# Gated cross-attention and FFN on one core: half of the first context group loaded from ScalarE's queue, context transposed ahead of x, and every engine's order table redrawn

## What is computed

```python
def reference(x, ctx_2048, mask_BxS2_bk0, g_xattn, g_ffn, L0_ffn_w_gating, L0_ffn_w_linear):
    def _L0_xattn_ref(hidden_states, memory_tokens, memory_mask):
        scale = 1.0 / jnp.sqrt(jnp.asarray(D, hidden_states.dtype))
        scores = jnp.einsum('bsd,bmd->bsm', hidden_states, memory_tokens) * scale
        scores = jnp.where(memory_mask[:, None, :], scores, neg_inf)
        attn = jax.nn.softmax(scores, axis=-1)
        readout = jnp.einsum('bsm,bmd->bsd', attn, memory_tokens)
...
    def _L0_ffn_ref(x, w_gating, w_linear):
        ff_gate = _qdot(x, w_gating[0])
        gate_value = jax.nn.gelu(ff_gate)
        ff1 = _qdot(x, w_gating[1])
        activations = gate_value * ff1
        outputs = _qdot(activations, w_linear)
        return outputs
    x = x + jnp.tanh(g_xattn[0]) * _L0_xattn_ref(_layernorm(x, axis=-1), ctx_2048, mask_BxS2_bk0)
    x = x + jnp.tanh(g_ffn[0]) * _L0_ffn_ref(_layernorm(x, axis=-1), L0_ffn_w_gating, L0_ffn_w_linear)
    return x
```

## Time and profile before

| | us |
|---|---|
| median of 3 runs | 126.36 (126.28 to 127.42) |
| the profiled execution, time | 127.25 |
| its span, first to last instruction | 125.50 |
| PE busy | 120.9 (96%) |
| DVE busy | 97.0 (77%) |
| ACT busy | 87.8 (70%) |
| POOL busy | 82.3 (66%) |

### The profile page before, as it was taken

One profiled execution on the slowest core, in us unless ns is written; L12 is line 12 of the kernel. 1 busy time (PEld: TensorE's weight loads), 2 busy tenths in 40 slices (PEclk: granted clock), 3 DMA queues, 4 the chain that ended last, 5 costly groups with the idle time before them and its releaser, 6 DMA issues.

```text
span 125.5 us, 2568 instructions
## 1 busy us (share of the span) xinstructions
PE 120.9 (96%) x863; PEld 104.2 (83%) x863; DVE 97.0 (77%) x210; ACT 87.8 (70%) x155; POOL 82.3 (66%) x143
## 2 busy tenths in 40 slices
...
GB/s 99 320 189 334 416 290 49 94 123 229 264 291 102 159 218 130 110 81 284 356 254 102 0 0 0 130 45 0 0 0 5 0 0 0 3 0 47 42 125 125
DMA packets 34440, 15.73 MB, mean 125 GB/s; under 512 B 26230, under 2 KB 33019, under 8 KB 34427
## 3 DMA queue, kind: packets, MB, share of 16 engines
...
HBM read 14.52 MB, written 1.05 MB: 124 GB/s over the span
## 4 chain that ended last, share of the span: by engine, by line
PE 66%; SPq 11%; DMA 10%; ACT 4%; issue 4%; DVE 3%; DVEq 0%; ACTq 0%
PE ring L774 13%; SPq L369 10%; DMA cn<-in_ctx_dram 8%; PE scores L854 6%; PE pv L825 6%; PE pv L833 6%; PE pv L829 6%; PE scores L788 6%; PE scores L791 6%; PE scores L792 6%; PE ring L870 6%; DMA raw<-in_ctx_dram 2%; ACT gate L575 2%; DVE ring L639 1%; PE scores L808 1%
## 5 line engine op out<-in xcount | busy, mean ns | idle before, releaser
L461 POOL TENSOR_TENSOR chl<-cn,chl 128x256 fp32r<-128x256 f32 (+1 forms) x52 | 37.8, 761 | 7.1 <-ACT chl L519 7.0
L645 DVE TENSOR_TENSOR pT_lo<-ring,pT_hi 128x512 fp32r<-128x512 f32 (+1 forms) x32 | 17.6, 578 | 6.9 <-ACT pT_hi L512 6.7
L512 ACT ACTIVATE pT_hi<-ring 128x512 fp32r<-128x512 f32 (+1 forms) x32 | 15.6, 513 | 8.3 <-PE ring L774 8.1
L645 DVE TENSOR_TENSOR cT_lo<-ring,cT_hi 128x512 fp32r<-128x512 f32 (+1 forms) x28 | 16.8, 624 | 4.5 <-ACT cT_hi L512 4.5
L792 PE MATMUL scores<-cT_hi,xT_lo 128*128 128x512 f32 (+2 forms) x60 | 20.1, 342 | 0.0
L791 PE MATMUL scores<-cT_lo,xT_hi 128*128 128x512 f32 (+2 forms) x60 | 20.0, 342 | 0.0
L469 POOL TENSOR_TENSOR ws<-ws,wc 128x256 f32<-128x256 f32 x24 | 15.4, 674 | 6.0 <-DVE wc L687 6.0
L825 PE MATMUL pv<-chl,pT_hi 128*128 128x256 f32 (+1 forms) x104 | 18.9, 294 | 0.0
L512 ACT ACTIVATE cT_hi<-ring 128x512 fp32r<-128x512 f32 (+1 forms) x28 | 14.6, 547 | 5.3 <-PE ring L774 3.2
L833 PE MATMUL pv<-chl,pT_lo 128*128 128x256 f32 (+1 forms) x104 | 17.5, 281 | 0.0
L829 PE MATMUL pv<-chl,pT_hi 128*128 128x256 f32 (+1 forms) x104 | 17.5, 280 | 0.0
...
## 6 DMA issues: line engine op xcount, KB each, us to landing
...
out_dram<-xs SPq DMA_DIRECT2D x8, 128.0 KB, 1.7
...
```

Of the source, the lines that this page charges most:

```text
L461: last = nc.gpsimd.tensor_tensor(chl[b % 2][0:parts, t, D:2 * D], cn[b % 2][0:parts, t, :], chl[b % 2][0:parts, t, 0:D].bitcast(f32), ALU. ...
L512: nc.scalar.activation(dst, bank_view(f, size), ACT.Copy).then_inc(hi_ready, 1)
L645: nc.vector.tensor_tensor(dst, bank_view(f, size), hi.bitcast(f32), ALU.subtract).then_inc(lo_ready, 1)
```

## The change

`WARM` goes from 14 to 12. The first half of the first context group, 256 KB, is issued by ACT as its first transfer instead of by SP as its third; SP keeps the second half. PE turns `C0:0` ahead of `X0:0`. All six tables (PE, ACT, DVE, POOL, SP and the banks) are redrawn. The instructions are the same ones, except the two filler matmuls. Of the tables, the diff below shows the first line of PE's and all of SP's.

```diff
-    WARM = 14
+    WARM = 12
...
     PE_ORDER = """
-        X0:0 C0:0 W2 X0:1 C0:1 W3 A1:0 A1:1 W4 C0:2 C0:3 A0:0 B0:0 A0:1 C0:4 C0:5 B0:1 S1:1 B0:3 B0:2 C1:1
+        C0:0 X0:0 W4 X0:1 C0:1 A1:0 W2 A0:0 W3 C0:2 C0:3 A1:1 A0:1 B0:0 C0:4 C0:5 B0:1 S1:1 C1:0 C0:6 C1:1
...
     SP_ORDER = """
-        X1 C1:0 W0 M1 C1:1 C1:2 X2 C1:3 T2:0 T2:1 W1 W2 M3 C2:0 C2:1 T2:2 W3 M2 C3:3 C2:3 T3:0 T3:1 C3:0
-        C2:2 C3:1 C3:2 W4 T3:2 W5"""
+        X1 C1:0 M1 C1:3 W0 C1:1 C1:2 X2 T2:1 W1 T2:0 W2 C2:0 C2:2 C2:3 T2:2 C2:1 M3 M2 T3:0 W3 C3:1 C3:2
+        T3:1 C3:0 W4 C3:3 T3:2 W5"""
...
-                    halves = [(t0, (t0 + t1) // 2), ((t0 + t1) // 2, t1)] if b == 0 and g == 0 else [(t0, t1)]
-                    for i, (a, z) in enumerate(halves):
-                        sp_eng.dma_start(cn[b % 2][:, a:z, :], rows[:, a:z, :]).then_inc(
-                            c00_in if i < len(halves) - 1 else c_in[b % 2][g], 16)
+                    if b == 0 and g == 0:
+
+                        t0 = (t0 + t1) // 2
+                    sp_eng.dma_start(cn[b % 2][:, t0:t1, :], rows[:, t0:t1, :]).then_inc(c_in[b % 2][g], 16)
...
+            half = GT // 2
+            actor.dma_start(cn[0][:, 0:half, :], ctx_2048[0, 0:NF * P, :].rearrange(
+                "(t p) d -> p t d" if 0 in by_block else "(p t) d -> p t d", p=P)[:, 0:half, :]).then_inc(c00_in, 16)
             actor.dma_start(mrow0, mask_BxS2_bk0[0:1, :]).then_inc(m0_in, 16)
```

More of the change, by code:

```diff
@@ L62, in gated_cross_attention_ffn @@
-        P5:2 S7:1 S7:2 N0 V5:0 P5:3 P6:1 V5:1 S7:3 N1 P6:0 P6:2 V5:2 V5:3 P6:3 H0 V6:0 V6:1 P7:0 P7:1 V6:2
-        V6:3 H1 P7:3 V7:0 P7:2 V7:1 V7:2 V7:3 H2 N2 H3 H4 H5 H6 N3 H7 H8 H9 H10 H11 Y0 H12 Y1 H13 H14 H15 Y2
+        C0:0 X0:0 W4 X0:1 C0:1 A1:0 W2 A0:0 W3 C0:2 C0:3 A1:1 A0:1 B0:0 C0:4 C0:5 B0:1 S1:1 C1:0 C0:6 C1:1
+        S0:1 B0:3 S0:2 B0:2 S0:3 C1:2 X1 C1:3 S1:2 S1:3 S2:0 C1:4 C1:5 P0:0 S2:1 S3:0 P0:3 P0:1 P0:2 V0:0
+        S3:1 C1:6 S2:2 P1:0 V0:1 S2:3 P1:1 V0:2 X2 V0:3 S3:2 S3:3 P1:2 S4:0 P1:3 V1:0 V1:1 P2:0 P2:1 P2:2
@@ L64, in gated_cross_attention_ffn @@
+        V1:2 V1:3 S5:0 P2:3 S4:1 S5:1 P3:1 P3:0 V2:0 V2:1 C2:6 V2:2 V2:3 P3:3 X3 S4:2 S4:3 P3:2 V3:0 V3:1
+        V3:2 V3:3 P4:1 P4:0 S5:2 S5:3 S6:0 V4:0 C3:6 P4:2 S6:1 P5:1 V4:1 V4:2 P5:0 N0 S6:2 P4:3 S6:3 S7:0
+        S7:1 V4:3 S7:2 N1 P5:2 S7:3 P5:3 V5:0 P6:3 P6:0 P6:1 V5:1 V5:2 V5:3 H0 P7:0 P6:2 V6:0 P7:2 V6:1 V6:2
+        P7:1 V6:3 H1 P7:3 V7:0 V7:1 V7:2 V7:3 H2 N2 H3 H4 H5 H6 N3 H7 H8 H9 H10 H11 H12 H13 Y0 H14 Y1 H15 Y2
         Y3 Y4 Y5 Y6 Y7"""
     ACT_ORDER = """
-        X0:0 C0:0 X0:1 C0:1 R0:0 C0:2 C0:3 R0:1 B0:0 C0:4 C0:5 B0:1 K1 B0:3 B0:2 C1:1 C1:0 C0:6 B1 X1 C1:3
@@ L69, in gated_cross_attention_ffn @@
[L69 to L72, removed]
+        C0:0 X0:0 X0:1 C0:1 R0:0 C0:2 C0:3 R0:1 B0:0 C0:4 C0:5 B0:1 R0:2 C1:0 C0:6 C1:1 B0:3 K1 B0:2 R0:3
@@ L73, in gated_cross_attention_ffn @@
+        C1:2 X1 C1:3 E0 R1:3 C1:4 C1:5 P0:0 B1 P0:3 P0:1 P0:2 E1 C1:6 R1:2 P1:0 C2:1 K2 P1:1 C2:0 R1:0 X2 E2
+        C2:3 P1:3 P1:2 R1:1 C2:2 P2:0 P2:1 P2:2 E3 C2:5 C2:4 R2:3 P2:3 R2:2 K3 C3:0 P3:1 P3:0 B2 C2:6 R2:1
+        P3:3 R2:0 X3 P3:2 E4 C3:1 C3:2 R3:0 P4:1 R3:2 C3:3 P4:0 E5 C3:6 P4:2 L0 P5:1 C3:4 C3:5 B3 R3:1 P4:3
+        P5:0 L1 R3:3 N0 E6 P5:2 P5:3 N1 P6:3 E7 P6:1 P6:0 P7:0 P6:2 H0 P7:2 P7:1 H1 P7:3 L2 H2 N2 H3 H4 L3
         H5 H6 N3 H7 H8 H9 H10 H11 H12 H13 H14 H15"""
     DVE_ORDER = """
-        G0:0 G0:1 X0:0 C0:0 X0:1 C0:1 C0:2 C0:3 G1 C0:4 C0:5 M1:0 W0 C1:1 C1:0 C0:6 M0:0 M0:1 X1 C1:3 C1:2
@@ L78, in gated_cross_attention_ffn @@
[L78 to L82, removed]
@@ L83, in gated_cross_attention_ffn @@
-        H13 H14 Y2 H15 Y3 Y4 Y5 Y6 Y7"""
+        G0:0 G0:1 C0:0 X0:0 X0:1 C0:1 C0:2 C0:3 G1 C0:4 C0:5 M1:0 C1:0 C0:6 C1:1 M0:0 W0 M0:1 X1 C1:2 C1:3
+        M1:1 G2 C1:4 C1:5 P0:0 G3 M2:0 P0:1 P0:3 W1 P0:2 C1:6 D2:1 D2:0 P1:0 C2:1 M2:1 M3:0 C2:0 P1:1 D2:3
+        X2 A0 C2:3 P1:3 D2:2 P1:2 C2:2 M3:1 P2:0 D2:5 P2:1 P2:2 D2:4 A1 C2:4 C2:5 P2:3 D3:0 W2 C3:0 P3:1 U0
+        P3:0 M4:0 A2 C2:6 M5:0 M4:1 P3:3 X3 P3:2 D3:1 D3:2 C3:1 C3:2 A3 D3:3 P4:1 M5:1 C3:3 P4:0 U1 U3 U2
+        C3:6 P4:2 D3:4 D3:5 P5:1 C3:4 C3:5 M6:0 W3 P5:0 M6:1 P4:3 A4 M7:0 P5:2 P5:3 M7:1 P6:3 P6:0 A5 P6:1
```

14 lines of the change are left out of this document (8 added, 6 removed).

## The result

The changed kernel takes 136.15 us (136.03 to 136.29 in 4 runs); the kernel before, run beside it, takes 126.41 (126.28 to 127.42). The ratio is 1.077, with a 95% interval from 1.072 to 1.081: slower by 9.7 us. The forecast was 131.0, with 132.6 as the upper end, so the direction was right and the size was not. The profiled execution has a span of 134.5 us, against 125.5. Two single executions further down were disturbed, 307.44 us in e3 and 421.39 us in e5, and are left out of their medians.

The account below looks back on a forecast made before the run. PE was taken to bound the kernel, busy 120.9 of 125.5 us. The terms -0.6 - 0.5 + 2.7 + 2.5 + 0.5 = +4.6 on the median 126.36 gave 131.0 us, range 127.5 to 132.6.

Parts of the forecast that it names:

- head: Start of PE: first context half lands earlier, second score unit reads ready parts; -0.6 us, between 0 and -1.0.
- the stall in the middle goes: PE's wait at 64.15 ends because ACT's context group is issued before `T2:2`; -0.5 us, bounds 0 and -0.6.
- `T2:2` late: SP's block load waits for `D2:2` to free `raw`, so PE stands at `P2:3`; +2.7 us, +2.1 to +3.5.
- `T3:0` late: Next block load, behind `C2:1` and two masks, makes PE stand at `C2:6`; +2.5 us, 0 to 3.2.
- late next: `M4:0` comes late on DVE, so PE waits at `S4:2`; +0.5 us, bounds 0 and 1.1.
- everything else that moved: POOL's low parts and ACT's bias of batch 1, later now, costed at nothing because PE's work covers them.
- the upper bound: Latest landing of the first context half issued by ACT: 3.40 us after 0.72, at 4.12; head then gives 0.
- the signs: What would show the forecast in traces: DVE and PE gaps, SP's wait ending near 43, second context group near 9.2.
- One stall only: Rival, chance 0.17: `T3:0` is there in time, only the `T2:2` stall stays; +1.6, 128.0 us.
- faster or the same: Rival, chance 0.15: `T2:2` is early enough; 125.3 us without any PE stall, 126 to 127 with half stall times.
- The change doesn't do what it says: Rival, chance 0.08: shared engines bring the half no earlier, x's turn is 0.4 later; head +0.4, 132.0 us.
- The lower clock: Rival, chance 0.06: TensorE stays longer at its lower level at the head, up to 1.5 us more; 132.5 us.

Follow-up runs that it names:

- e3: Changed kernel with DVE's product `fo` written as tensor_scalar (`seen` as scalar operand) instead of tensor_tensor; 132.09 us, ratio 1.045.
- e5: Kernel before with only the new head: ACT issues the first context half, 12 fillers, `C0:0` ahead of `X0:0`; 126.44 us, ratio 1.002.
- e11: e4 with the head of before put back, so only the redrawn tables behind it are left of the change; 126.48 us, ratio 1.003.
- e4: Changed kernel with `T2:0` loaded ahead of `T2:1` on SP and `fo` as tensor_scalar; 126.63 us, ratio 1.0024.
- e3b: Same kernel as e3 in a second set of runs, made for a profile; 131.85 us, ratio 1.044.
- e8: Changed kernel with POOL waiting for its own last result behind each context group of batch 2, `fo` unchanged; 131.82 us, ratio 1.044.
- e10: Changed kernel with `T2:0` loaded ahead of `T2:1` on SP and the POOL waits of e8, `fo` unchanged; 126.30 us, ratio 1.001.
- e1: Changed kernel with only SP's two loads exchanged, `T2:0` ahead of `T2:1`; median 129.07 us, ratio 1.012 from two of six runs.
- e2: Changed kernel with SP issuing `C2:1`, `M3` and `M2` before `T2:2` instead of between it and `T3:0`; 134.88 us, ratio 1.064.
- e6: Kernel before with only ACT issuing the first context half, 14 fillers and all orders as before; 127.93 us, ratio 1.010.

## Why the prediction was wrong in size and right in direction

| step of the forecast | forecast | measured |
|---|---|---|
| head | -0.6 | -0.66 in the trace of after; 0 in the times (e5, e11 against e4) |
| the stall in the middle goes | -0.5 | -0.55 against the profiled run of before; 0 in the times |
| `T2:2` late | +2.7 | +2.95 |
| `T3:0` late | +2.5 | +2.25 |
| late next | +0.5 | +0.8 |
| everything else that moved | 0 | +2.4, and +1.6 for the lower clock behind it |

In the traces the measured terms sum to 8.8; another 0.2, in small pieces towards the end, makes the 9.0 between the spans.

**What held.** The block buffer was read rightly, down to its sizes. The wait of SP ended at 43.13 (43.2 was forecast, "near 43"), DVE stood 3.48 us before the turn from `raw` at 49.93 and 3.75 before the turn from `act` at 58.35 (3 and 4 us, at 46 to 50 and 55 to 59), PE stood at `P2:3` and at `C2:6`. The three terms sum to 5.7 in the forecast and 6.0 in the trace. In the times they are 131.85 - 126.63 = 5.2 (e3b against e4) or 131.82 - 126.30 = 5.5 (e8 against e10), of which some is now clock and not gap, since in e3b and e8 TensorE fell to its lower level behind the first gap and the second gap shrank for it. At the head the half was ready at 0.72 + 3.21 = 3.93, between the 3.8 taken and the 4.12 of the upper bound, and the second group came at 9.16, where the signs had asked for 9.2:

```profile
0.72 3.21 DMA cn<-in_ctx_dram
```

```profile
9.16 1.04 PE L777 MATMUL ring<-ident,cn 128*128 128x128 f32 x8
```

**The step that failed** is the sentence "Everything else that moved (POOL's low parts, ACT's bias of batch 1, later now) I cost at nothing". It was backed by PE's cover between a tile's last score and its first softmax fill, which asks whether each engine has time for its own work. It did not ask whether two engines get in each other's way. What moved is in POOL's table: `Z2:0 Z2:3 Z2:1 Z2:2` now stand next to each other, and the first of them waits for the last of ACT's four high parts, so that all are there when POOL starts, and thirteen instructions run without a break, in e1 and e2 as well. That held one DVE instruction for 3.65 us, DVE's next turn with it, ACT's high parts behind that (ACT idle for 2.40 us, released by the turn), and PE's `V4:0`. Worth 4.3 us in the times (136.15 - 131.85), it is the larger part of the miss of 5.2.

The Trainium skill describes this kind of meeting ("SBUF — State Buffer", section "SBUF: two separate sides"): VectorE and GpSimd share a pair of ports, a VectorE instruction with two SBUF inputs counts as a user against a GpSimd instruction that reads SBUF, and the one that comes first holds it "for the whole instruction" while the other is blocked. The runs agree on who collides: `fo` with two tensors is held, and with a scalar operand it is not (0.21 us in the same place). They agree only in part on how long. By that rule `fo` is let in at the end of the POOL instruction that is running, after at most the 0.75 us of one. So it went in the seven other meetings of before and after, each of which ended within 0.02 us of the end of a POOL instruction; but in the run of 13 it was held over five further ones (four in e1 and in e2).

**The rest of the miss** is the -1.1 of gains. The head's 0.66 and the stall's 0.55 are both in the traces, but the other runs show neither as a gain in time. The stall of the earlier trace rows stood in one profiled run that lay 0.9 us above its median; e5 and e6, whose tables are the same in the middle, have no such wait. The head scatters by about as much as it gained. Without these two the forecast would have been 132.1, against the 131.85 of e3b, which has only the foretold gaps; that these agree so closely is in part luck, since e3b's clock behind the first gap, which nobody had priced, stands in for most of its second gap. A term of half a microsecond that is read from one execution should have been given to the range, not to the sum.

**The rivals.** "One stall only" and "faster or the same" fell to DVE's two waits. "The change doesn't do what it says" was right in half: the half came earlier (3.93 for 5.02), and x's first tile 0.73 later (3.62 for 2.89), which PE's new order hid. The lower clock came, but in the changed kernel behind the third gap and not at the head (there it lasted long in the profiled runs of e1 and e6); the forecast had put no price on a clock that falls after a wait in the middle.
